# One slot later for the inverted sums, 32 columns for the transposed shifts, slot 14 for an image's first qk product

## The reference

```python
qkv = einsum('bnc,oc->bno', tokens(group_norm(x)), qkv_w)     # 1024 x 576 an image
attn = softmax(einsum('bhnd,bhmd->bhnm', q, k) * 32 ** -0.5)   # 6 x 1024 x 1024
out = einsum('bhnm,bhmd->bhnd', attn, v)                       # heads joined to 192 channels
y = x + (einsum('bnc,oc->bno', out, proj_w) + proj_b)
```

## Time and profile before

| | |
|---|---|
| runs | 1485.42, 1489.29, 1489.77 us; median 1489.29 |
| profiled execution | 1487.5 us, span 1485.7 us |
| busy PE, weight loads | 1417.9 us (95%), 634.1 (43%) |
| busy DVE, ACT, POOL | 1160.2 (78%), 1194.7 (80%), 1313.9 (88%) |
| granted TensorE clock, mean | 0.986 |

### The profile page before, as it was taken

How to read it: one execution, slowest core, us unless ns; L and a number is a source line. 1 busy time by engine, 2 the same in 40 slices (tenths; PEclk the granted TensorE clock), 3 DMA queues, 4 the chain that set the end, 5 groups by cost and what they waited for, 6 DMA issues and landing times.

```text
span 1485.7 us, 51069 instructions
## 1 busy us (share of the span) xinstructions
PE 1417.9 (95%) x22044; PEld 634.1 (43%) x22044; DVE 1160.2 (78%) x2008; ACT 1194.7 (80%) x1999; POOL 1313.9 (88%) x639
## 2 busy tenths in 40 slices
PE   3799999999999999999999999999999999999986
PEld 1234444444444444444444444444444444453332
DVE  4788788788888878887887788778878887877822
ACT  2278897988889797888979788797988979787774
POOL 4169998999989999998999899898999989989993
PEclk9799999999999999999999999999999999999999
DMA  4313151423526152251514226261332414131202
GB/s 109 65 45 89 38 117 46 104 44 84 100 59 113 49 98 50 78 105 59 113 49 96 52 73 111 59 110 29 99 72 65 91 48 92 38 95 39 73 17 86
DMA packets 88729, 110.02 MB, mean 74 GB/s; under 512 B 38968, under 2 KB 51384, under 8 KB 88504
## 3 DMA queue, kind: packets, MB, share of 16 engines
q1 hardware_dynamic: 88504, 106.76, 31.6%
HBM read 42.71 MB, written 13.14 MB: 38 GB/s over the span
## 4 chain that ended last, share of the span: by engine, by line
PE 60%; ACT 12%; DMA 8%; SPq 7%; POOL 7%; DVE 3%; issue 3%; DVEq 0%; POOLq 0%; ACTq 0%
PE max_ps L537 16%; PE scores_ps L537 15%; PE heads_ps L657 14%; PE extra_ps L537 9%; ACT probs L802 7%; PE extra_ps L615 6%; DMA sums_spread<-sums_sb 6%; SPq L429 5%; POOL prob_pairs L869 4%; POOL prob_pairs L875 2%; ACT qk_hi L727 2%; DVE half_max L968 1%; ACT xhat_a_hi L765 1%; SPq L365 1%; DVE qk_lo L1002 1%
## 5 line engine op out<-in xcount | busy, mean ns | idle before, releaser
L968 DVE TENSOR_REDUCE half_max<-max_ps 128x1 f32<-128x512 f32 x1536 | 981.7, 682 | 193.2 <-PE max_ps L537 174.5
L802 ACT ACTIVATE probs<-scores_ps,exp_scale 128x512 f32<-128x512 f32 x1536 | 967.1, 696 | 158.9 <-PE scores_ps L537 147.8
L869 POOL TENSOR_TENSOR prob_pairs<-probs 128x1024 f32<-128x1024 f32 x380 | 892.9, 2378 | 83.4 <-ACT probs L802 83.1
L537 PE MATMUL max_ps<-k_stack,q_stack 96*32 96x512 f16 x6144 | 624.3, 385 | 16.9 <-DVE half_max L968 12.1
L537 PE MATMUL scores_ps<-q_stack,k_stack 98*32 98x512 f16 x6144 | 617.9, 381 | 8.4 <-ACT probs L802 8.0
L657 PE MATMUL heads_ps<-probs,v_sb 128*32 128x512 f32 x3072 | 404.1, 595 | 2.3 <-ACT probs L802 1.0
L537 PEld LDWEIGHTS max_ps<-k_stack,q_stack 96*32 96x32 f16 x6144 | 181.2, 96 | 327.2 <-DVE half_max L968 156.4
L537 PEld LDWEIGHTS scores_ps<-q_stack,k_stack 98*32 98x32 f16 x6144 | 181.3, 96 | 177.7 <-ACT probs L802 59.6
L875 POOL TENSOR_TENSOR prob_pairs<-prob_pairs 128x1024 f32<-128x1024 f32 x96 | 226.1, 2379 | 0.0
L615 PE MATMUL extra_ps<-prob_pairs,ones 128*32 128x512 f32 x1128 | 140.0, 592 | 0.0
L657 PEld LDWEIGHTS heads_ps<-probs,v_sb 128*32 128x32 f32 x3072 | 100.8, 110 | 69.4 <-issue 13.6
(11 more groups left out here) (139 smaller groups left out, 936.6 us busy)
## 6 DMA issues: line engine op xcount, KB each, us to landing
q_stack<-qk_hi SPq DMA_DIRECT2D x96, 128.0 KB, 3.9
k_stack<-qk_hi SPq DMA_DIRECT2D x96, 128.0 KB, 5.0
inv_sb<-inv_rows SPq DMA_DIRECT2D x47, 256.0 KB
x_sb<-x SPq DMA_DIRECT2D x16, 512.0 KB, 6.6
x_sb<-x SPq DMA_DIRECT2D x32, 256.0 KB, 7.7
x_res<-x SPq DMA_DIRECT2D x16, 512.0 KB, 3.8
out<-x_res SPq DMA_DIRECT2D x15, 512.0 KB, 3.2
q_stack<-qk_lo SPq DMA_DIRECT2D x48, 128.0 KB, 3.9
```

The source lines that it names most:

```text
L537: last = pe.matmul(to[at:at + D, :], weights[:, at:at + D], moving, start=start, stop=stop)
L802: nc.scalar.activation(probs[:, a, s % RING, HALF * half:HALF * (half + 1)], scores_ps[:, u_bank(s, u), :], ACT.Exp, scale=exp_scale[:, 0: ...
L869: nc.gpsimd.tensor_tensor(prob_pairs[:, a, q, :], probs[:, a, (s - 1) % RING, :], probs[:, a, s % RING, :], ALU.add).then_inc(pairs_added, 1)
L968: nc.vector.tensor_reduce(half_max[:, a, tile, half:half + 1], max_ps[:, bank, :], AX_X, ALU.max).then_inc(max_read[bank], 1)
```

## The change

Five constants move work in the tables, one tile gets 32 columns instead of 16, and one memset is added. `XHAT_AT` is read in order, so its last three pieces move: one from slot 7 to 9, one within slot 9, one from 9 to 10. `INVERTED`, `INV_SPREAD` and `INV_GATHERED` move by one slot for all three pairs: to 14, 15, 16 for the first, 22, 23 and slot 0 of the next step for the second, and 6, 7, 8 of the next step for the third. `SUMS_SPREAD` and `DIVIDED` stay. `HEADS_UNIT` goes from 3 to 2: ACT copies the heads after the third exponential. The diff, cut to its changed lines:

```diff
-XHAT_AT = ((3, 3), (4, 1), (5, 3), (6, 1), (6, 3), (7, 3), (9, 1), (9, 3))
+XHAT_AT = ((3, 3), (4, 1), (5, 3), (6, 1), (6, 3), (9, 1), (9, 3), (10, 1))
...
-QK_SLOTS = (12, 15, 19)
+QK_SLOTS = (14, 15, 19)
...
-INVERTED = TILES + 5
-INV_SPREAD = TILES + 6
-INV_GATHERED = TILES + 7
+INVERTED = TILES + 6
+INV_SPREAD = TILES + 7
+INV_GATHERED = TILES + 8
...
-VALUES_UNIT, HEADS_UNIT = 2, 3
+VALUES_UNIT, HEADS_UNIT = 2, 2
...
-        neg_max = sb("neg_max", [P, 2 * TILES], F32)
+        neg_max = sb("neg_max", [P, D], F32)
...
-                    last = pe.transpose(extra_ps[0:2 * TILES, 0:P], neg_max[:, :], ident[:, :])
+                    last = pe.transpose(extra_ps[0:D, 0:P], neg_max[:, :], ident[:, :])
...
+            nc.vector.memset(neg_max[:, :], 0.0)
...
-                        nc.vector.tensor_reduce(neg_max[:, :],
+                        nc.vector.tensor_reduce(neg_max[:, 0:2 * TILES],
```

## The result

The changed kernel is slower: 1530.45 us (median of 6 runs, 1527.78 to 1537.19) against 1488.87 (6 runs, 1485.19 to 1489.77), a ratio of 1.0285, 95% interval 1.0265 to 1.0305. Its profiled execution, with a span of 1535.4, lies at the upper end of its runs, so the profile shows 49.7 us more span where the medians differ by 41.6.

The account below looks back on a forecast made before the run. No engine total decides, so slots 12 to 16 were read for PE's waits: 13.49 + 0.2 + 0.2 - 0.2 = 13.69 against 14.27, 6.4 us; slot 21 gains 3, second pair loses 1.5; net -8, 1481 us, range 1468 to 1496.

Parts of the forecast that it names:

- the landing of `inv_sb`: Second and third pair: the transfer was priced at 5.0 us from issue to landing, from a row at 1459.00.
- one of the signs of being wrong: Wrong if reciprocals wait over 1 us in the mean, heads_out waits for inv_sb in slot 10, or slot 12 stays 3.7.
- The same delay touches POOL: Third pair: inv_sb issued about 2.7 later, landing at 727 to 728.5, hidden or 0.5 late for heads_out; 0.2 us a step.
- Second pair's reciprocal: inv_sb moves past write_norm to 779.9, lands at 784.9, POOL wants it at 783.81; 0.1 us a step lost.
- SP stands longer in slot 8: Rival: inv_rows lands late behind six transfers, stopping POOL, ScalarE, then PE in 14 steps; about 1501 us, chance 0.16.
- Slots 12 to 16: Moving the qk product and reciprocal makes slots 12 to 15 sum to 13.49 us, against a mean of 14.27.
- The 0.2 for the sums: Slots 12 to 15: 0.2 us added for steps where sums_spread lands later than the 1.9 us left free.
- Transposes of 32 columns: Slots 13 and 21: the weight load runs ahead and PE stops less; 0.2 us saved, bounds 0 and 0.31.
- The rival figure of an ordinary f32 product: If the 32-column transpose runs as an ordinary f32 product, the gain would be 0.1 us instead of 0.2.
- Heads copied one exponential earlier: Slot 0 may gain up to 0.22 us, slot 16 lose 0.1 to 0.2; net 0, bounds -0.2 and +0.2 a step.
- Normalisations: The last moves into slot 10, about 1.95 us later, and stays covered by 0.5 us on POOL; no effect.

Follow-up runs that it names:

- pair0: The changed kernel with the inversion one slot later for the first pair only, second and third pair at their old slots; 1479.36 us.
- mm32: pair0 with the transpose of the 32 columns written as an ordinary f32 product of neg_max with the identity; 1473.69 us.
- oldxhat: pair0 with the eight normalisations where they were before the change; 1478.24 us.
- mm16: mm32 with 16 columns of neg_max instead of 32 in the ordinary f32 product; 1475.16 us.

## Why the prediction was wrong

**The step that failed: the landing of `inv_sb`.** The prediction priced it at 5.0 at both places, from the earlier trace rows. That row is from the end of the span, with little else on the queues. In place it is 6.8 for the second pair and 8.6 for the third (step 8); the terms taken as 0.1 and 0.2 a step cost 1.9 and 1.8. So `heads_out` waits for `inv_sb`, which is one of the signs of being wrong that the prediction named.

*The same delay touches POOL.* All but the landing was right, and the lateness shows in slot 11 before it reaches slot 12. Slot 8 starts at 716.71 in step 7 of before and at 829.10 in step 8 of after, 112.39 apart. On the clock of before, `inv_sb` is issued at 834.24 - 112.39 = 721.85, where the prediction's 719.24 + 2.7 gives 721.9; but POOL goes on at 842.82 - 112.39 = 730.43, not at 727 to 728.5. So POOL is 1.8 late against 728.67, and slot 11 grows by 1.8 in the mean. The term was taken as 0.2. The page gave a bound that was not used: POOL did not wait there before, which says only that the landing took at most 728.67 - 719.24 = 9.4. With 2.6 of delay, any landing over 6.8 comes late. The 9.7 of the earlier trace rows, for a transfer issued a little later in the same step, should have been one end of the range. And the trace of before held a landing at this very place. Its waits have two of `heads_out` for `inv_sb`; one is that of the earlier trace rows, the other is the third pair's in step 14 (waits of the whole span, then SP and POOL):

```profile
POOL heads_out L854 <- DMA inv_sb<-inv_rows: 5.2, 2, 2.7
...
1329.69 0.59 SPq L481 DMA_DIRECT2D inv_sb<-inv_rows  x1
...
1338.25 1.28 POOL L854 TENSOR_TENSOR heads_out<-heads_sb,inv_sb 128x512 f32<-128x512 f32 x1 [2.65 <-DMA inv_sb<-inv_rows]
```

That is 8.6 from issue to consumer, with the six transfers of `stack_pair(0)` just ahead and those of `stack_pair(1)` just behind. Priced with it, the third pair would have come out 1.8 late. The DMA share of 835 to 845 in the changed kernel (packets, MB, share of the 16 engines) shows how full it is:

```profile
q1 hardware_dynamic: 747, 1.59, 94.1%
```

At the issue itself the engines are nearly idle (9% from 834.2 to 836.0), and the six transfers of `stack_pair(1)` follow 0.65 behind. The load of x is not what makes the landing slow: in steps 12 and 13 SP has none there, and it takes 9.0 and 9.4. That the six transfers do is read from this and not tried: no run took them away.

*Second pair's reciprocal.* The issue was right as well: 804.05, less 23.80 (slot 1 starts at 801.39 and at 777.59), is 780.25, where 779.9 was forecast. The landing is 1.8 longer than priced, so POOL stands idle for 2.85, where the prediction had it 1.1 late. Taken 0.1; slots 3 and 4 together cost 1.39 + 0.53 = 1.92 a step. That is nearly all of ScalarE's wait of 2.08, so 0.1 out of a wait of 0.3 to 0.5 looks too little as well. Full engines are not the reason here. From 804 to 811 the same view as above says:

```profile
q1 hardware_dynamic: 787, 0.32, 21.3%
```

`norm_rows` (`write_norm`) goes 0.66 ahead of this `inv_sb`. In step 14 of the changed kernel there is no `write_norm`, POOL does not wait, and the transfer has landed within 6.1. That points at `write_norm`, but why the landing gets longer behind it stays open.

With what the two late landings cost in the slots in place of its two terms, the prediction's sum comes out at 1481 + (1.8 - 0.2) x 14 + (1.9 - 0.1) x 13 = 1527.

*The rival "SP stands longer in slot 8"* had the right victim and chain (POOL, ScalarE, PE in 14 steps) but the wrong cause: `inv_rows` has landed when SP issues `inv_sb`, at 834.24 - 112.39 = 721.9, within the 721.5 to 722 of the forecast. It is the transfer after it that is slow.

*Slots 12 to 16.* Right. In `pair0` slots 12 to 15 are 3.18, 2.93, 3.69, 3.69, in sum 13.49, the figure of the prediction before corrections. The 0.2 for the sums was not needed: in the changed kernel `sums_spread` is issued 844.66 - 112.39 - 730.53 = 1.7 later, where 2.7 was forecast, and the reciprocals wait for 1.3 us in all. In the changed kernel slot 12 is 3.40, still late from slot 11.

*Transposes of 32 columns.* Wrong: 0.2 was taken, nothing came. The load stands 0.84 alone as before, slot 13 is 2.94, slot 21 2.93. It was the lower bound, "if a transpose is always alone", and `mm32` shows that the transpose as such is the reason. The Trainium skill (TensorEngine Tiling (Array Packing), Key Properties) has the drain at a change of tiling mode. The prediction read 16 columns beside 32 as such a change; the traces do not agree that this was the stop, since 32 columns keep it and the 16 columns of `mm16` are free of it. Whether the transpose itself counts as a change of mode, no run shows. Nor does the transpose run as an ordinary f32 product, as the prediction thought possible: it is one matmul (48 in the span), the product of `mm32` two (96). The rival figure of an ordinary f32 product, 0.1 a transpose, was low: 0.21.

*Heads copied one exponential earlier.* Net 0 was taken; slot 0 gains 0.17 (bound 0.22), and slot 16 loses nothing (2.81 against 2.84). All versions with the old `HEADS_UNIT` keep 2.90 in slot 0; the constant was not tried alone.

*Normalisations.* Right: `oldxhat` has the same slots.

*Left out:* at the close, the last pair's later inversion stands open. The wait of `heads_out` for `inv_sb` there is 9.8, where it was 2.55, and the stretch behind the last group is 2.9 longer.

## What to carry to other kernels

Price a moved transfer by the stretch it moves into: the slack is its consumer's start less its issue before, the cost what is left after the delay, and a landing read where little else moves is the lower end only. Look in the waits for the same transfer at the same place: here one step of the kernel before had it. A wait that is moved in an in-order DMA list moves behind everything that stands there, so when a slot later looks free on the compute engines, read that list first; and a delay that gains one consumer (the first pair) can be taken by that one alone. Where a transpose stands in a dense stream of matmuls, an ordinary product with the identity can be cheaper (here by 0.21 us a slot).

## What the runs showed of the hardware

A 128-column f32 transpose keeps PE to itself, with 16 columns and with 32 (its weight load 0.84 us after the one before it). The same product without the transpose mode has its weights loaded while the matmuls before it run, though it takes two passes, and shortens the slot by 0.21 us. The same 256 KB broadcast from DRAM took 5.0 us near the end of the span, and 6.8 and 8.6 in two stretches of one step, from the issue to the start of what waits for it. How busy the DMA engines are does not explain the 6.8: their share was 24% from 1459 to 1464, 21% from 804 to 811, and 94% from 835 to 845.
